# A transformer block on one core, two batches in turn: rebuilt as one pipeline over four chunks of 512 queries

## The reference, cut to what matters

```python
def L0(x, c, mask):                       # B=2, N=1024, C=256, H=16 heads of D=16
    shift1, scale1, gate1, shift2, scale2, gate2 = split(silu(c @ ada1_w + b) @ ada2_w + b, 6)
    q, k, v = (x @ qkv_w).reshape(b, n, 3, H, D)
    attn = softmax(where(mask, q @ k.T * D ** -0.5, -inf))     # mask is set only past each batch's length
    a = (attn @ v) @ proj_w + proj_b
    x = x + gate1 * (ln(a) * (1 + scale1) + shift1)
    m = gelu(x @ fc1_w + fc1_b) @ fc2_w + fc2_b                # 256 -> 1024 -> 256
    return x + gate2 * (ln(m) * (1 + scale2) + shift2)

def L1(x, t):
    shift, scale, gate, shift_f, scale_f, gate_f = split(silu(t) @ ada_w + ada_b, 6)
    h = gelu((ln(x) * (1 + scale) + shift) @ ssm_w1 + b) @ ssm_w2 + b       # 256 -> 256 -> 256
    x = x + gate * h
    h = gelu_tanh((ln(x) * (1 + scale_f) + shift_f) @ ff_w1 + b) @ ff_w2 + b  # 256 -> 512 -> 256
    return x + gate_f * h
```

## Time and profile before

| | before |
|---|---|
| median of three runs | 544.06 us (541.18 to 549.45) |
| profiled execution, first to last instruction | 551.6 us |
| PE, DVE, POOL, ACT busy | 409.4, 275.8, 232.5, 189.7 us |
| TensorE clock granted, mean | 0.862 |
| DMA moved | 31.22 MB |

### The profile page before, as it was taken

One profiled execution on the slowest core, in us unless ns is written; L12 is line 12 of the kernel. 1 busy time (PEld: TensorE's weight loads), 2 busy tenths in 40 slices (PEclk: granted clock), 3 DMA queues, 4 the chain that ended last, 5 costly groups with the idle time before them and its releaser, 6 DMA issues.

```text
span 551.6 us, 7211 instructions
## 1 busy us (share of the span) xinstructions
PE 409.4 (74%) x2137; PEld 299.3 (54%) x2138; DVE 275.8 (50%) x527; ACT 189.7 (34%) x272; POOL 232.5 (42%) x242
## 2 busy tenths in 40 slices
PE   1274878868877898957782726899897688986686
PEld 1161444434456796845672525554445587776575
DVE  7242564775516807386410325567543933839720
ACT  1220033533630444322541200456462333432433
POOL 7671053880001646656445890000000454846643
PEclk9998576985987699997997775699797889997999
DMA  7569627411000000000027395131100000000001
GB/s 252 139 225 156 148 70 182 89 31 30 2 1 1 1 0 2 2 1 1 0 77 214 113 186 100 31 56 35 31 2 1 1 1 1 1 1 1 1 14 63
DMA packets 20804, 31.22 MB, mean 57 GB/s; under 512 B 5319, under 2 KB 13053, under 8 KB 20492
## 3 DMA queue, kind: packets, MB, share of 16 engines
q1 hardware_dynamic: 18366, 22.15, 17.3%
q0 software_dynamic: 2384, 8.42, 5.3%
HBM read 22.89 MB, written 7.37 MB: 55 GB/s over the span
## 4 chain that ended last, share of the span: by engine, by line
issue 52%; POOL 31%; DMA 6%; PE 3%; DVE 3%; SPq 2%; ACT 1%; POOLq 1%; ACTq 0%; DVEq 0%
POOL hid L614 12%; POOL x_tok L600 6%; POOL rstd L609 3%; DMA stage<-in_L_cond_ssm_w 3%; DMA probs<-in_L_cond_ada_w 3%; POOL ff_hi L582 2%; POOL ff_lo L590 2%; POOL stage L587 2%; POOL veps L607 1%; DVE probs L764 1%; PE ps L1054 1%; PE ps L1034 1%; SPq L401 1%; POOL ssm_lo L590 1%; POOL ssm_hi L582 1%
## 5 line engine op out<-in xcount | busy, mean ns | idle before, releaser
L857 DVE TENSOR_REDUCE mmax<-ps 128x2 f32<-128x512 f32 x128 | 82.4, 686 | 48.8 <-PE ps L1169 48.8
L614 POOL TENSOR_TENSOR hid<-probs,hid 128x512 fp32r<-128x512 f32 x56 | 73.5, 1320 | 52.1 <-ACT hid L755 51.7
L607 POOL TENSOR_TENSOR veps<-mv,eps 128x2 f32<-128x2 f32 x32 | 8.0, 250 | 189.0 <-DVE mv L909 188.7
L1169 PE MATMUL ps<-ka,qa 96*128 96x256 f32 x256 | 63.6, 372 | 24.9 <-DMA qa<-q_dram 19.1
L721 ACT ACTIVATE probs<-ps 128x1024 f32<-128x1024 f32 x64 | 63.2, 1024 | 54.9 <-PE ps L1190 54.9
L1169 PEld LDWEIGHTS ps<-ka,qa 96*128 96x128 f32 x256 | 51.0, 245 | 47.7 <-DVE mmax L857 22.9
L1034 PE MATMUL ps<-fc_hi,hid 128*128 128x256 f32 x256 | 53.2, 293 | 5.9 <-POOL hid L614 5.4
L808 DVE TENSOR_TENSOR actA_lo<-ps,actA_hi 128x512 fp32r<-128x512 f32 x20 | 13.4, 689 | 84.0 <-ACT actA_hi L679 84.0
L1190 PE MATMUL ps<-qa,ka 98*128 98x512 f32 x128 | 50.1, 483 | 5.8 <-DMA qa<-m_rows 3.9
L1034 PEld LDWEIGHTS ps<-fc_hi,hid 128*128 128x128 f32 x256 | 43.0, 197 | 10.8 <-issue 6.1
L600 POOL TENSOR_TENSOR x_tok<-x_tok,vec 128x1024 f32<-128x1024 f32 x16 | 38.1, 2384 | 7.3 <-PE ps L1067 5.4
(11 more groups left out here) (172 smaller groups left out, 829.6 us busy)
## 6 DMA issues: line engine op xcount, KB each, us to landing
qa<-q_dram SPq DMA_DIRECT2D x48, 128.0 KB, 3.9
probs<-in_L_cond_ada_w SPq DMA_DIRECT2D x2, 1536.0 KB, 12.5
x_tok<-in_x SPq DMA_DIRECT2D x4, 512.0 KB, 6.7
stage<-in_L_cond_fc_w POOLq DMA_DIRECT2D x8, 256.0 KB, 3.6
vec<-mod_dram POOLq DMA_DIRECT2D x2, 1024.0 KB, 7.4
stage<-in_L_cond_ff_w POOLq DMA_DIRECT2D x4, 512.0 KB, 7.6
q_dram<-actC_hi SPq DMA_DIRECT2D x6, 256.0 KB, 3.8
q_dram<-actC_lo SPq DMA_DIRECT2D x6, 256.0 KB, 4.6
```

The source lines that it names most:

```text
L614: pool.tensor_tensor(hid[:, n % HSLOTS, 1, :], gelu_out[:, n % 2, :], hid[:, n % HSLOTS, 0, :].bitcast(F32), ALU.subtract).then_inc(s_h_lo, 1)
L857: dve.tensor_reduce(mmax[:, u % 2, h * T + 2 * tp:h * T + 2 * tp + 2], bank.rearrange("p (t n) -> p t n", t=2), axis=AX.X, op=ALU.max).the ...
L1169: last = pe.matmul(ps[:, bank, t * p.keys:(t + 1) * p.keys], qa[0:ROWS_S1, slot, h, q0:q0 + P], kav[0:ROWS_S1, (u % NG) * HG + h, :], star ...
```

## The change: one pipeline over four chunks

The path for 256 keys becomes a program of its own (`pipelined`), with no loop; the general path stays for other masks, with its attention order unskewed. The choice is made once, before either path starts.

- **Order.** `ORDER` is one list of steps from which every engine writes its queue. A prologue does the attention of chunk 0. Then `stage(m)` does the layers of chunk m and, between them, the attention of chunk m+1. The last stage has no attention.
- **Halves.** Norms, transposes and layers work on 256 tokens (`h` is 0 or 1). An `up` makes two 128-channel tiles by 256 tokens in one bank, two GELUs and one rounding evacuate it, and a `dn` takes 12 matmuls. Matmul counts of the MLP: 12 of 256 columns for `up` instead of 6 of 512, `dn` as before.
- **Two heads per operand.** `qa` and `ka` hold two heads, one from partition 0 and one from partition 64 (49 to 51 rows each). `s1` and `s2` issue the two heads' matmuls one after the other, into different banks. `exp` is one instruction for each bank (128 x 512) instead of one for two banks.
- **PSUM.** Five banks are a ring that all steps share in the order of the list; two hold the sums of `dn` and `proj`, one `pv`.
- **Modulation.** Weights of ssm and ff are split once, unmodulated. The scale is applied as T2 and T3 are evacuated (two ACT and two DVE instructions of 256 instead of one each of 512), the gate when the sum is taken (`y`). The biases of proj and fc2 come as matmuls with a row of ones. The products that normalise (`z`) and the residual sums (`res`) move to POOL.
- **Loads.** ACT's queue issues the weight loads; x of the second batch is loaded early and kept.

```diff
+def attention(a, g, fill):
+    fill = list(fill) + [[]] * 8
+    steps = [("s2", a, g, 0, 0)] + fill[0] + [("s2", a, g, 0, 1)] + fill[1] + [("s2", a, g, 1, 0)] + fill[2]
+    steps += [("pv", a, g, 0)] + fill[3] + [("s2", a, g, 1, 1)] + fill[4] + [("pv", a, g, 1), ("o", a, g)] + fill[5]
+    steps += [("qa", a + 1, g)] * (a + 1 < CHUNKS) + [("ka", 1, g)] * (a == 1)
+    return steps + [("oT", a, g)] + fill[6]
...
+def prologue():
+    steps = [("x", 0, 0), ("x", 0, 1), ("q", 0, 0), ("q", 0, 1), ("qa", 0, 0)]
+    steps += [("x", 1, 1), ("k", 0, 0), ("k", 0, 1), ("ka", 0, None), ("qa", 0, 1), ("v", 0, 0), ("v", 0, 1), ("qa", 0, 2), ("qa", 0, 3)]
+    steps += [("ada1",), ("x", 1, 0), ("q", 1, 0), ("q", 1, 1)]
+    steps += s1_steps(0, 0) + [("ada", 0), ("mT", 0, 0)]
+    steps += s1_steps(0, 1) + [("load2",), ("mT", 0, 1)]
+    steps += attention(0, 0, [[s] for s in s1_steps(0, 2)]) + [("mT", 0, 2), ("mod", 0)]
+    steps += attention(0, 1, [[s] for s in s1_steps(0, 3)]) + [("mT", 0, 3), ("ada", 1), ("load3",)]
+    steps += attention(0, 2, []) + [("mod", 1)] + attention(0, 3, [])
+    return steps + [("shift", 1, 0, 0), ("shift", 1, 0, 1), ("O", 0, 0), ("O", 0, 1), ("upb",)]
...
+    steps = [("proj", m, 0), ("proj", m, 1)]
+    steps += [("bn", 1, m, 0), ("rstd", 1, m, 0), ("cen", 1, m, 0), ("bn", 1, m, 1), ("rstd", 1, m, 1), ("upd", 1, m, 0),
+              ("cen", 1, m, 1), ("upd", 1, m, 1)]
+    if m == 0:
+        steps += [("x", 2, 0), ("x", 2, 1), ("q", 2, 0), ("q", 2, 1)]
+    if m == 1:
+        steps += [("x", 3, 0), ("q", 3, 0), ("q", 3, 1)]
+    steps += some(4)
+    steps += [("T1", m, 0), up("fc", m, 0, 0)] + some(1) + [up("fc", m, 0, 1), ("T1", m, 1)] + some(1)
+    steps += [("shift", 2, m, 0), ("shift", 2, m, 1)]
+    steps += [up("fc", m, 0, 2), dn("fc", m, 0, 0)] + some(1) + [up("fc", m, 0, 3), dn("fc", m, 0, 1)] + some(1)
+    steps += [up("fc", m, 1, 0), dn("fc", m, 0, 2)] + some(1) + [up("fc", m, 1, 1), dn("fc", m, 0, 3)]
+    steps += norm_after(2, m, 0)[:3] + some(1) + norm_after(2, m, 0)[3:]
+    steps += [up("fc", m, 1, 2), dn("fc", m, 1, 0)] + norm_before(3, m, 0) + some(2) + [up("fc", m, 1, 3), dn("fc", m, 1, 1)] + some(2)
+    if m == 0:
+        steps += [("x", 3, 1), ("k", 1, 0), ("k", 1, 1), ("v", 1, 0), ("v", 1, 1)]
+    steps += some(2)
+    steps += unit(0, [[dn("fc", m, 1, 2)], late[:], [dn("fc", m, 1, 3)] + norm_after(2, m, 1)[:3], norm_after(2, m, 1)[3:]])
+    steps += norm_before(3, m, 1)
+    steps += [("T2", m, 0), up("ssm", m, 0, 0)]
+    ssm_a = [dn("ssm", m, 0, 0), ("y", "ssm", m, 0), ("res", "ssm", m, 0)] + norm_before(4, m, 0)
+    steps += unit(1, [[], ssm_a])
+    steps += [("T2", m, 1), up("ssm", m, 1, 0)]
+    ssm_b = [dn("ssm", m, 1, 0), ("y", "ssm", m, 1), ("res", "ssm", m, 1)] + norm_before(4, m, 1)
+    steps += unit(2, [[], ssm_b])
+    steps += [("T3", m, 0), up("ff", m, 0, 0), up("ff", m, 0, 1), dn("ff", m, 0, 0)]
+    ff_a = [dn("ff", m, 0, 1), ("y", "ff", m, 0), ("res", "ff", m, 0), ("out", m, 0)]
+    steps += unit(3, [[], ff_a])
+    steps += [("T3", m, 1), up("ff", m, 1, 0), up("ff", m, 1, 1)]
+    steps += [("O", a, 0)] * more + [dn("ff", m, 1, 0)] + [("O", a, 1)] * more + [dn("ff", m, 1, 1)]
+    steps += [("shift", 1, a, 0), ("shift", 1, a, 1)] * more
+    return steps + [("y", "ff", m, 1), ("res", "ff", m, 1), ("out", m, 1)]
...
+            elif kind == "s2":
+                _, a, g, kt, p = step
+                n = AT[step]
+                if unit(a, g) and p == 0:
+                    act.wait_ge(s_pv, KT * (unit(a, g) - 1) + kt + 1)
+                for e in range(2):
+                    act.wait_ge(s_s2, n + 1)
+                    act.activation(probs[:, kt, 2 * p + e, :], ps[:, bank(step, e), :], ACT.Exp, scale=SCALE).then_inc(s_exp, 1)
```

2719 lines of the change are left out of this document (1721 added, 998 removed).

## The result

The changed kernel takes 628.65 us (median of four runs, 623.92 to 632.36) against 544.28; the ratio is 1.154, with a 95% interval of 1.146 to 1.163. The forecast was 562, with a range up to 612. The direction was the likeliest of the three; the time lies above the range, and above the 625 up to which rival 2 reached.

A forecast was written before the change was run, and what follows sets the result against it. PE led, busy 409.4 of 551.6 us, the rest waits, low clock and start. Prologue 112, three stages of 124 and last stage 86 gave 570, scaled to the runs' median 562, with a range from 490 to 612.

The forecast's parts named there:

- rival 2: PE's clock falls in the attention units: 12 to 15 us a stage more, 600 to 610; chance 0.20 including table-load drain.
- the price of the clock: Each of three stages: 118 us at full clock, plus 6 (between 3 and 12) at clock 0.83, making 124.
- 14 + 31 + 69.6: A stage at full clock: start 14 (17.7 on average), fc 31, attention units and end 69.6, with unit 0 at 9.2.
- the first `s1`: Prologue: first s1 at 45 us instead of 53.6, from the second batch's 29 us after first transposes at 16.
- the last stage: Last chunk's layers with no attention between them: 84 us, with clock 86.
- The sum's first term: Prologue, start to stage 0: first s1 at 45, then reductions 15, four units, two modulation products, 7 more; 112 us.
- The chain of the units: Attention unit with half of ssm (g=1, g=2): serial chain of ACT and PE, 15.3 us, PE working about 8.
- Unit 3's 18.4: Stage's last attention unit: a second up and a dn waiting for POOL ahead of its s2; 18.4 us.
- the end's 11.4: Stage's end: T3, two up, load, GELU, rounding, low part, O, two dn; 11.4 us.
- The rule of a drain: Table loads on ACT: a drain of about 1.38 us per switch would add 34 us, 597; chance 0.08.
- Two heads per operand: s2 pairs in attention: at most 14 us saved over the kernel; 0 to 5 taken, none counted.
- removing the 40 us: Stretch between batches: its 40 us are saved and given back; per chunk 124 us against 129.

The follow-up runs named there:

- run 5: Changed kernel with 376 extra matmuls (constant operands, output unchanged) where PE waits; 587.65 us, ratio 1.074 to the kernel before the change.
- run 12: run 10 plus s1 behind fc's first up product, matmuls ahead of T1, last-stage halves overlapping, bias rows behind x's first low part; 577.64 us, ratio 1.062.
- run 14: run 12 with the four s1 steps in front of T1 again; 559.82 us, ratio 1.023 to the kernel before the change.
- run 10: run 9 plus extra matmuls ahead of the prologue's s1 steps and of fc's first up product; 566.66 us, ratio 1.041.
- run 13: Changed kernel with normalising products and residual sums moved from POOL to DVE; 639.24 us, ratio 1.167 to the kernel before the change.
- run 2: run 1 plus up products of ssm and ff between the exponentials; 581.34 us, ratio 1.064; 573.56 and 577.74 us at the higher clock.
- Run 4: Changed kernel with each GELU of the new path replaced by Relu (29 table loads go, output differs); 617.77 us, ratio 1.128.
- run 7: Changed kernel with each s1 matmul issued twice into the same place; 635.73 us, ratio 1.161 to the kernel before the change.
- run 18: run 17 without the extra matmuls; 566.85 us median of six, 554.10 and 554.96 at the higher clock, against 546.07 for the kernel before the change.
- run 17: run 14 with units overlapping: next unit's T2 or T3 and first s2 pair ahead of the second pv; 559.25 us, ratio 1.027.
- run 9: Changed kernel with the edits of run 2 and run 5 together; 566.32 us, ratio 1.046 to the kernel before the change.
- run 16: Kernel before the change with extra matmuls ahead of each pv and of the s1 steps of each batch's first unit; 554.02 us, ratio 1.011.
- run 1: Changed kernel with down products of ssm and ff behind their unit's last s2 pair, not ahead of the third; 631.65 us, ratio 1.154.

## Why the prediction was wrong

**In short.** The step that failed is the price of the clock: 6 us a stage in the sum, and nothing in the prologue. Without that term the sum has 14 + 31 + 69.6 = 114.6 us for stage 2. With the clock brought up and the same order of steps (run 5) that stage took 112.6; at the clock that the changed kernel was granted it took 126.4. So the chain was sized rightly, and the term is 13.8 us there in place of 6. Two smaller steps failed beside it, the first `s1` and the last stage.

**The sum's first term, the prologue (112, measured 134.5).** Two parts of it failed. The first `s1` at 45 us was taken from the second batch's 29 us, as if products followed the first transposes as there. At the start they follow the split of the weights: x was transposed at 11.03, and the first product came at 29.75, behind a low part of x that stood behind DVE's rows of biases:

```profile
26.01 2.28 DVE L609 TENSOR_TENSOR p_bias_hl<-p_o_tok,p_qk_buf 1x512 fp32r<-1x512 f32 x1
28.32 1.29 DVE L632 TENSOR_TENSOR p_x_lo<-ps,p_x_hi 128x512 fp32r<-128x512 f32 x2
```

The first `s1` came at 54.5, 9.5 late. Moving the bias rows brought it to 50.1 and 50.5 (runs 12 and 14); the rest of the delay stands ahead of them, where DVE waits for the high part of the weights and splits off the low one (21.54 to 23.4 us); no run moved that. What follows the first `s1`, 67 us forecast, took 80, and I had given the prologue no term for the clock at all. It ran at 0.61; with extra matmuls (run 5) the same queues took 69.8 at 0.79.

**The chain of the units was right at full clock.** 15.3 was forecast for a unit with half of ssm; run 5 has 15.0 and 14.0 at 1.00, the changed kernel 15.5 at 0.89 and 17.7 at 0.62. Unit 3's 18.4 is 17.6 in run 5 and 19.7 to 20.6 in the changed kernel, the end's 11.4 is 11.5 and 13.6. The start of stage 2 took 12.9 against 14, those of stages 0 and 1, with the next chunk's projections, 22.9 and 20.4 against 19.5. fc took 29.7 us against 31 and unit 0 15.9 against 9.2, but that unit holds the last two s1 steps with their waits of 0.7 us and two of fc's down products; the two together were 45.6 against 40.2, and 41.6 in run 5.

**The clock's term was the one that failed in the stages.** I took 6 us a stage, from a clock of 0.83 and "between 3 and 12". The clock was 0.80 on the mean, not far from what I took; what it cost was more. Run 5 brought back 5.6, 9.9 and 13.8 us a stage, at clocks of 0.88, 0.90 and 0.95. Even by my own numbers 6 was low: 45 us of PE's work on the chain at a mean clock of 0.83 take 45/0.83, 9 us more. And a mean hides that the clock fell on the units, where the chain is: to 0.62 over a whole one. Rival 2 had the mechanism, the place and a price of 12 to 15 us a stage, with 0.20, though it waited for a mean clock of 0.75; it also left out the prologue, which is worth another 10 us.

**The last stage (86, measured 94.5).** Two causes can be named, and no run splits them: `z` takes 2.43 us a half on POOL, where I had written 0.7, and the clock was 0.77. With more clock the same order took 92.5 (0.87, run 5) and 89.8 (0.90, run 10). Moving `z` and `res` to DVE, right where they stood in the list, didn't help (run 13).

**Table loads.** 32 loads ran in the changed kernel, 1.28 us each, as forecast. The rule of a drain that the prediction weighed (the Trainium skill, ScalarE: Activation LUTs, What ACT_TABLE_LOAD costs) doesn't show: the load at 212.47 begins 0.02 us behind the end of the rounding, and the exponential starts at 213.76, as it ends. The same holds for the loads of run 2's unit, GELU included. Run 4 took 29 of the 32 loads away for 11 us, less than the 37 of the loads themselves.

**Two heads per operand.** I counted nothing for it, between 0 and 5 us. PE's part is real: the first eight matmuls of s1 take 1.22 us at half clock, as four did before, so PE has half the time for s1. Most of s1 lies beside DVE's reductions; what shows of it is about the 7 us that run 7 cost when it gave that time back, nearly all of them in the prologue.

```profile
54.54 1.22 PE L825 MATMUL ps<-p_ka,p_qa 49*128 49x256 f32 x8 [7.12 <-issue]
```

**What removing the 40 us did.** As forecast, it was given back: stages of 126 to 137 us against the 129 us a chunk of the kernel before. The largest piece of the give-back was shown: it is the place of one up product and its GELU in each unit, two in unit 3 (50 us, run 2), some 18 to 25 by order and the rest by the clock that came with it. What keeps the best versions, 560 (run 14) and 554 to 555 (run 18 at its higher clock), still about 2% above the kernel before was tested by no run. A drain at the table loads isn't it. For POOL's share and the s1 steps one other place each was tried, for overlapping units one order. The windows say where the time is: in run 18 the stages take 102 to 119 us a chunk, less than the 129 of the kernel before, but the prologue and the last stage, in which a chunk's attention and a chunk's layers stand alone, take 129.8 and 92.1 of the 552.4 us.

## What to carry to other kernels

When two jobs share the queues, write out for each engine what it does while the other's result is on its way, and put independent work (here four exponentials) into the longest way, before the instruction that waits. A chain that PE walks in turns with others has to be priced at the clock that such a chain gets, and the prologue too; and before a wait is taken away, look which engine is the bound in the place where the work then goes: the four s1 steps were free at the stage's start and cost 13 to 19 us in fc. Extra matmuls in PE's waits are a quick test of how much a low clock costs, and what they give is a lower bound: 41 us here, where PE waited; less than nothing in the kernel before and in run 17's order, where PE had few waits and the matmuls made the units longer. Once the order is mended, take them out again and measure.

## What the runs showed of the hardware

- 376 matmuls of no use made a kernel 6.5% faster, with the mean clock at 0.891 in place of 0.786. Where PE already worked, 256 doubled matmuls left the clock at 0.786. At a clock of 1.00 the same kind of matmuls made units 0.5 to 1.8 us longer (runs 9, 16 and 17).
- Matmuls of 49 rows on partitions 0 and 64, issued in turn into two banks, overlapped: eight in 1.22 us at half clock and in 0.74 at full, where four of 96 rows had taken 1.22.
- Small DVE instructions were dear while POOL split weights. The 1x512 cast took 1.39 us in the changed kernel, begun 0.15 us behind a subtraction of POOL and ended 0.28 behind its end, and 1.48, 1.39 and 1.39 us with the same 0.27 to 0.28 in runs 1, 2 and 5. In runs 14 and 18 a like cast, into another tile, fell between two instructions of POOL and took 0.42. The 1x512 subtraction beside POOL's cast took 2.28, where two 128x512 subtractions take 1.29. That DVE waited for POOL there fits all of these; no run tested it by itself.
